# Two-layer gated cross-attention and feed-forward on one core: the negated mean moves to VectorE, the first feed-forward looks three tiles ahead instead of four, six chunks of the last weights are signed during the convolution, and loads change their places

## The chip, the cores and the metric

The kernel runs on one core of a Trainium2 chip. The core has TensorE (PE, matmuls), VectorE (DVE), ScalarE (ACT), GpSimd (POOL) and SyncE (SP, which here only issues DMA transfers); each runs its own instruction stream, and they meet by semaphores. The metric is the device time of one execution in microseconds (us).

## The reference, cut to what matters

`x` is 8x256x512, `ctx` has the same shape. Four residual steps follow each other:

```python
x = x + tanh(g_xattn[0]) * ssm_conv(ctx, ctx, layernorm(x), taps, D)      # causal conv of the pair products k_i*v_j, times q, summed over i
x = x + tanh(g_ffn[0])   * bitnet_ffn(layernorm(x), w1, w2, w3)           # hidden 1408, rows quantised to 8 bits, weights to {-1,0,1}/scale
x = x + tanh(g_xattn[1]) * masked_softmax_attention(layernorm(x), ctx)    # one head, 256 keys a batch
x = x + tanh(g_ffn[1])   * one_bit_ffn(layernorm(x), w1, w2, w3)          # hidden 2048, groups of 64 quantised, weights sign(w)*mean|w|
```

`layernorm(x) = (x - mean) / sqrt(var + 1e-5)` over the last axis. The mean of the absolute weights is over a whole matrix.

## The kernel before, in words

`x` lives on chip as 16 tiles of 128x512 (`x_sb[:, n, :]`). The four residual steps are four stages, each a loop over 16 tiles: the **convolution** (`n` = 0..15), the **first feed-forward** (`t` = 0..15), the **attention** (`i` = 0..15) and the **last feed-forward** (`n` = 0..15). Every engine has one stream, written out by hand in the order in which it runs; nothing reorders it, so a wait holds back everything behind it on its engine. Stages overlap only where the streams say so: the first tiles of a stage are prepared in the last steps of the stage before.

**Layer norm.** `ln_sums` (VectorE, L276 statistics and L278 aggregate, written as mean and variance), `ln_root` (GpSimd, L282 and L285) and, outside the convolution, `ln_norm` (GpSimd, L290, one 128x512 tensor_scalar that subtracts the mean and multiplies by the root). The convolution's own norm is on ScalarE (L867).

**Convolution.** For tile n, SyncE loads the filter matrices (`load_toeplitz`, L324, from `kpad`), x (L316) and the context heads (`load_context`, L313). GpSimd forms the pair products (`pairs`, L485 of 128x1536 and L488 of 128x256). TensorE runs two times 20 matmuls (L627) for a tile, transposes q (L615) and the result (L622). ScalarE's `copy_q` (L850, L852) takes the transposed q out of PSUM; in `conv(n)` TensorE turns q for n+1, and some 14 matmuls later it needs its copy. VectorE folds (L1069 to L1084). Beside it ScalarE takes the first feed-forward's weights in chunks: the absolute sums (`sum_weight`, L878, at the steps of `ABS_STEP`) and the ternary values (`ternary`, L885 and L888, at `TERN_STEP`).

**First feed-forward.** For tile t: three chunks of up-matmuls (L690, 24 instructions), their SiLU on ScalarE, `a_product` on VectorE (L1119), then quantising (`a_scale_h`, L1125), rounding, a DMA transpose, and 11 down-matmuls (L702). Its input is prepared ahead: `a_stats` (L276), `a_norm` (L290), `a_scale_x` (L1099 to L1106), `a_round_x`, `a_integers_x` (L521), `turn_x` (a DMA transpose). The order of these in the loop is t+4 for `a_stats` and `a_norm` and t+3 for `a_scale_x`.

**Last weights.** 24 chunks of 128x1024 are loaded by SyncE (`load_b`, L362) into two buffers, and ScalarE's `sign_b` writes the signs (L915) and the sum of the absolutes (L917). It begins in the fifth step of the first feed-forward and goes on through the attention, one a step, to the first steps of the last feed-forward.

**Attention.** For tile i: transposes (L713), scores (L724, from `load_rows` and `ctxT`), softmax with ScalarE's L926 and L933, readout (L746). Layer norm and input of the last feed-forward's first three tiles are also prepared here.

**Last feed-forward.** For tile n: 64 up-matmuls (L763), 32 down-matmuls (L780). The input of tile n+1 is prepared within step n: `fb_scale_x`, `fb_round_x`, `fb_deq_x`, `fb_high_x`, `fb_low_x`, and SyncE's `fb_turn_x` (L444, DMA transpose).

## Time and profile before

| what | value |
|---|---|
| median of 3 runs | 732.27 us (729.6 to 733.1) |
| the profiled execution | 732.03 us |
| its span in the trace | 730.2 us |
| busy: TensorE, VectorE, ScalarE, GpSimd | 693.4, 607.0, 372.4, 326.7 us |
| granted TensorE clock, mean | 0.993 |

A timeline row gives the start in us from the span's beginning, the length of the group in us, the engine, the line of the program, output and input, the count, and in brackets the idle time ahead of it with what ended it. "Busy" of one engine says how much it had to do, and not how much of that the others waited for.

### The profile page before, as it was taken

To read this page: it belongs to the slowest core of one execution; us is meant where nothing else is said; L and a number is where in the kernel's file an instruction comes from. 1 tells how busy PE (TensorE), PEld (TensorE's weight loads), DVE (VectorE), ACT (ScalarE), POOL (GpSimd) and SP (SyncE) were. 2 spreads that over 40 slices of the span, in tenths; PEclk is the share of its full clock that TensorE was granted. 3 is DMA by queue.
4 is the path that set the end of the run, shared out by engine and by line. 5 is a ranking of instruction groups with operands and counts; after the bars stand their busy time and mean duration, and the time that the engine had idled before them with its cause. 6 is when DMAs were issued, how large, how long until landed. Compare 5 with 4: busy or idle time off the path is not lost.

```text
span 730.2 us, 9410 instructions
## 1 busy us (share of the span) xinstructions
PE 693.4 (95%) x3162; PEld 388.4 (53%) x3162; DVE 607.0 (83%) x1094; ACT 372.4 (51%) x541; POOL 326.7 (45%) x362
## 2 busy tenths in 40 slices
PE   5999999988889999899989999999999999999897
PEld 3777777766534444466664444444444444444343
DVE  3998888898899998756985899988888888898871
ACT  3255976281366668546887644443444334433430
POOL 5679788878787665467870002211011111110000
PEclk9999999999999999999999999999999999999999
DMA  8563363320046878979554433334223343332133
GB/s 281 195 242 127 107 247 129 116 78 10 7 113 163 161 166 171 206 252 389 169 145 116 101 73 88 84 76 83 56 63 75 86 88 88 72 87 65 37 73 101
DMA packets 140288, 90.97 MB, mean 125 GB/s; under 512 B 118992, under 2 KB 118992, under 8 KB 140240
## 3 DMA queue, kind: packets, MB, share of 16 engines
q1 hardware_dynamic: 138512, 86.35, 44.1%
q0 software_dynamic: 1200, 3.93, 1.6%
q8 instruction: 25, 0.41, 0.2%
q14 instruction: 23, 0.19, 0.1%
q10 hardware_dynamic: 528, 0.09, 0.1%
HBM read 53.04 MB, written 8.47 MB: 84 GB/s over the span
## 4 chain that ended last, share of the span: by engine, by line
PE 65%; DVE 18%; POOL 6%; DMA 4%; ACT 4%; issue 3%; SPq 0%; POOLq 0%; ACTq 0%; DVEq 0%
PE psum L763 26%; PE psum L627 18%; PE psum L780 14%; DVE phase_space L1119 3%; DVE a_scalars L1125 3%; POOL phase_space L290 3%; PE psum L724 2%; PE psum L746 2%; DVE ln_bn L276 2%; DVE a_scalars L1106 1%; DMA phase_space<-in_L_weights 1%; DVE a_scalars L1099 1%; DVE x_sb L1137 1%; DMA x_sb<-x_between 1%; PE psum L615 1%
## 5 line engine op out<-in xcount | busy, mean ns | idle before, releaser
L763 PE MATMUL psum<-phase_space 128*128 128x512 f16 x1024 | 225.3, 381 | 3.9 <-DMA phase_space<-phase_space 3.2
L627 PE MATMUL psum<-phase_space 128*128 128x288 f32 x640 | 165.3, 414 | 14.3 <-DVE phase_space L1258 8.8
L763 PEld LDWEIGHTS psum<-phase_space 128*128 128x128 f16 x1024 | 100.2, 98 | 127.4 <-issue 4.7
L627 PEld LDWEIGHTS psum<-phase_space 128*128 128x128 f32 x640 | 121.3, 194 | 47.2 <-issue 8.8
L602 POOL DMA_DIRECT2D out<-x_sb x15 | 9.5, 630 | 293.9 <-DVE x_sb L1251 293.9
L780 PE MATMUL psum<-phase_space 128*128 128x512 f16 x512 | 112.6, 379 | 0.0
L290 POOL TENSOR_SCALAR phase_space<-x_sb,ln_ag,ln_rs 128x512 f32<-128x512 f32 x48 | 101.2, 2108 | 9.1 <-POOL ln_rs L285 7.4
L690 PE MATMUL psum<-phase_space 128*128 128x512 bf16 (+1 forms) x384 | 79.2, 361 | 4.7 <-DVE phase_space L1119 4.3
L780 PEld LDWEIGHTS psum<-phase_space 128*128 128x128 f16 x512 | 50.1, 98 | 60.4
L1024 ACT ACTIVATE phase_space<-psum,b_scalars 128x512 f32<-128x512 f32 x64 | 43.2, 681 | 74.6 <-PE psum L763 74.2
L1030 ACT ACTIVATE phase_space<-phase_space,magic 128x1024 f32<-128x1024 f32 x32 | 36.5, 1148 | 84.8 <-DVE phase_space L1230 84.8
L1218 DVE SCALAR_TENSOR_TENSOR phase_space<-psum,b_scalars,phase_space 128x512 f32<-128x512 f32 x64 | 47.6, 747 | 27.1 <-ACT phase_space L1024 26.4
L690 PEld LDWEIGHTS psum<-phase_space 128*128 128x128 bf16 x384 | 37.1, 98 | 45.4 <-DVE phase_space L1119 4.4
L1069 DVE TENSOR_TENSOR phase_space<-psum,phase_space 128x1024 f32<-128x1024 f32 x32 | 39.1, 1222 | 16.8 <-PE psum L627 16.6
L485 POOL TENSOR_TENSOR phase_space<-phase_space 128x1536 f32<-128x1536 f32 x16 | 48.6, 3040 | 3.5 <-DMA phase_space<-in_context_heads 3.5
L1173 DVE TENSOR_REDUCE phase_space<-phase_space 128x8 f32<-128x512 f32 (+1 forms) x32 | 47.3, 1479 | 0.6
L276 DVE BATCH_NORM_STATS2 ln_bn<-x_sb 128x6 f32<-128x512 f32 x64 | 43.4, 679 | 3.0 <-DMA x_sb<-x_between 2.9
L702 PE MATMUL psum<-phase_space 128*128 128x512 bf16 x176 | 41.2, 383 | 1.8 <-DMA phase_space<-phase_space 1.8
L1243 DVE TENSOR_TENSOR phase_space<-phase_space 128x512 f16<-128x512 f32 x64 | 39.8, 684 | 0.0
L1237 DVE SCALAR_TENSOR_TENSOR phase_space<-phase_space 128x1024 f32<-128x1024 f32 x32 | 37.8, 1223 | 1.3
L285 POOL TENSOR_TENSOR ln_rs<-ln_ve,neg_half 128x1 f32<-128x1 f32 x64 | 36.2, 566 | 5.3
L282 POOL TENSOR_SCALAR ln_ve<-ln_ag 128x1 f32<-128x1 f32 x64 | 13.2, 206 | 56.3 <-DVE ln_ag L278 54.0
(110 smaller groups left out, 1013.3 us busy)
## 6 DMA issues: line engine op xcount, KB each, us to landing
phase_space<-in_L_weights SPq DMA_DIRECT2D x24, 512.0 KB, 4.6
phase_space<-in_L_weights SPq DMA_DIRECT2D x12, 704.0 KB, 7.0
phase_space<-kpad SPq DMA_DIRECT2D x14, 512.0 KB, 4.1
phase_space<-in_context_heads SPq DMA_DIRECT2D x16, 384.0 KB, 4.8
x_sb<-in_x_tiles SPq DMA_DIRECT2D x16, 256.0 KB, 4.6
phase_space<-in_context_turned SPq DMA_DIRECT2D x8, 512.0 KB, 6.2
x_between<-x_sb SPq DMA_DIRECT2D x16, 256.0 KB
x_sb<-x_between SPq DMA_DIRECT2D x16, 256.0 KB, 6.1
```

The lines of the kernel that those rows point to most:

```text
L276: nc.vector.bn_stats(ln_bn[:, stage, n % 2, :], x_sb[:, n, :]).then_inc(s_ln[stage], 1)
L290: nc.gpsimd.tensor_scalar(dst, x_sb[:, n, :], ln_ag[:, stage, n, 0:1], ln_rs[:, stage, n:n + 1], ALU.subtract, ALU.mult).then_inc(s_done, 1)
L485: nc.gpsimd.tensor_tensor(at(kv_k, E, [[NP, rows], [E, 3], [1, E]]), at(cx_sb[k], 0, [[EX, rows], [0, 3], [1, E]]), at(cx_sb[k], 1, [[EX, ...
L627: last = nc.tensor.matmul(at(bank(4 * hh + lo), 0, [[64, B], [1, NP]]), toep[n % 2][:, hh, (lo - li) * P:(lo - li + 1) * P], kv[n % 2][:, ...
L690: last = nc.tensor.matmul(bank(UPA[c][part])[:, 0:w], fa_qT[t % 4][:, kk, :], a_wT[part][:, kk, c0:c0 + w], start=(kk == 0), stop=(kk == L ...
L702: last = nc.tensor.matmul(bank(6 + t % 2), fa_hT[t % 2][:, c, :], a_wT[2][:, c, :], start=(c == 0), stop=(c == JA - 1))
L763: last = nc.tensor.matmul(bank(2 * (m % 3) + w), fb_qT[n % 2][:, kk % 2, kk // 2, :], b_wT[w][:, kk // 2, c * 512:(c + 1) * 512], start=(k ...
L780: last = nc.tensor.matmul(bank(6 + k), fb_hT[k][:, part, c, :], b_wT[2][:, c, :], start=(c == 0 and part == 0), stop=(c == JB - 1 and part ...
L1024: nc.scalar.activation(fb_s[m % 2], bank(2 * (m % 3)), ACT.Silu, scale=fb_sm[:, n % 4, 2:3]).then_inc(g_si, 1)
L1173: nc.vector.tensor_reduce(gx[:, 0, :], grouped(src), AX.X, ALU.max, apply_absolute_value=True).then_inc(s_steps, 1)
L1218: nc.vector.scalar_tensor_tensor(fb_h[n % 2][:, c * 512:(c + 1) * 512], bank(2 * (m % 3) + 1), fb_sm[:, n % 4, 3:4], fb_s[m % 2], ALU.mult ...
L1243: nc.vector.tensor_tensor(fb_tp[n % 2][:, 1, g * 512:(g + 1) * 512], fb_t[n % 2][:, g * 512:(g + 1) * 512], fb_tp[n % 2][:, 0, g * 512:(g ...
```

## The change

1. `ln_nm`, the negated mean, is a third instruction of `ln_sums` on VectorE (128x1), for all stages but the convolution's; `ln_norm` then adds it and multiplies by the root, instead of subtracting the mean and multiplying.
2. The second pair product of tile 0 goes from GpSimd to VectorE. The filter pad's store moves behind the first loads. One sum of absolute weights goes from step 5 to step 4.
3. The first feed-forward prepares `a_stats` and `a_norm` three tiles ahead (before: four) and `a_scale_x` two (before: three); the last half fold of the convolution stands behind the first two products.
4. Six of the 24 chunks of the last weights are loaded at n = 9 to 15 of the convolution and signed in its steps 10, 11, 14 and 15. The other 18 keep two buffers and move earlier; none is left for the last feed-forward.
5. SyncE: `turn_hidden` ahead of `turn_x`, `load_rows(4)` and `load_rows(5)` earlier, the last chunks among `fb_turn_x`.
6. In the last feed-forward, the input of tile 15 is scaled at the end of step 13 and finished in the first half of step 14.

```diff
         def ln_sums(dve, stage, n):
+            done = LN_STEPS[stage] * n
...
+            if stage > 0:
+                dve.wait_ge(s_ln[stage], done + 2)
+                nc.vector.tensor_scalar(ln_nm[:, stage, n:n + 1], ln_ag[:, stage, n, 0:1], -1.0, None, ALU.mult
+                                        ).then_inc(s_ln[stage], 1)
...
-            nc.gpsimd.tensor_scalar(dst, x_sb[:, n, :], ln_ag[:, stage, n, 0:1], ln_rs[:, stage, n:n + 1],
-                                    ALU.subtract, ALU.mult).then_inc(s_done, 1)
+            nc.gpsimd.tensor_scalar(dst, x_sb[:, n, :], ln_nm[:, stage, n:n + 1], ln_rs[:, stage, n:n + 1],
+                                    ALU.add, ALU.mult).then_inc(s_done, 1)
...
+        ABS_STEP[1, 2] = 4
...
+        NBF = 6
+        B_STEP = {10: (0,), 11: (1, 2), 14: (3, 4), 15: (5,)}
...
                     if n + 2 < NT:
                         load_toeplitz(n + 2)
+                    for q in {9: (0, 1), 11: (2,), 12: (3, 4), 15: (5,)}.get(n, ()):
+                        load_b(q)
...
                 for t in range(NT + 1):
+                    if t >= 1:
+                        turn_hidden(t - 1)
                     if t < NT - 2:
                         turn_x(t + 2)
-                    if t >= 1:
-                        turn_hidden(t - 1)
...
-                load_b(6)
-                load_b(7)
+                load_rows(4)
+                load_b(13)
+                load_rows(5)
...
+                load_b(21)
                 fb_turn_x(0)
-                load_b(2 * PERW + 1)
+                load_b(22)
                 fb_turn_x(1)
-                for j in range(2 * PERW + 2, NBC):
-                    load_b(j)
+                load_b(23)
                 fb_turn_x(2)
...
                     if n >= NT - 3:
                         a_round_x(n + 3 - NT)
+                    for q in B_STEP.get(n, ()):
+                        sign_b(q)
...
                 for t in range(NT):
                     a_silu(t, 0)
                     if t >= 1:
                         a_round_h(t - 1)
                     a_silu(t, 1)
-                    if t < NT - 3:
-                        a_round_x(t + 3)
+                    if 1 <= t < NT - 2:
+                        a_round_x(t + 2)
...
-                    if i >= 3:
-                        sign_b(i + 3)
+                    if 4 <= i < 15:
+                        sign_b(i + 9)
...
-                        if NT + 3 + NCB * n + c < NBC:
-                            sign_b(NT + 3 + NCB * n + c)
...
                 for t in range(NT):
                     a_product(t, 0)
+                    if 1 <= t < NT - 2:
+                        a_scale_x(t + 2)
+                    a_product(t, 1)
+                    if t < NT - 3:
+                        a_stats(t + 3)
                     if t == 0:
-                        a_product(0, 1)
                         fold_heads(NT - 1, 1)
-                    if t < NT - 3:
-                        a_scale_x(t + 3)
-                    if t >= 1:
-                        a_product(t, 1)
-                    if t < NT - 4:
-                        a_stats(t + 4)
                     a_product(t, 2)
...
+                    if n == NT - 3:
+                        fb_scale_x(NT - 1)
+                        fb_up_scales(NT - 1)
```

What this makes of ScalarE's stream around the convolution's tiles 11 and 12. Before, behind the copy of q for tile 12 (its last two rows are ahead of the first shown) follow the norm, the copy of the result, and directly the copy of q for tile 13:

```order
L860 ACTIVATE phase_space<-phase_space 128x64x8 [waits conv_summed,context_loaded0]
L867 ACTIVATE phase_space<-x_sb,ln_off,ln_rs 128x512 [waits conv_x_transposed,conv_offset_done]
L874 ACTIVATE phase_space<-psum,gates 128x512 [waits residual0_done,result_transposed]
L850 ACTIVATE phase_space<-psum 128x64x8 [waits products_folded,conv_x_transposed]
L852 ACTIVATE phase_space<-psum 128x64x4
L860 ACTIVATE phase_space<-phase_space 128x64x8 [waits conv_summed,context_loaded1]
L867 ACTIVATE phase_space<-x_sb,ln_off,ln_rs 128x512 [waits conv_x_transposed,conv_offset_done]
L874 ACTIVATE phase_space<-psum,gates 128x512 [waits residual0_done,result_transposed]
L885 ACTIVATE phase_space<-phase_space,magic,a_inv 128x1408 [waits a_means]
```

After the change, from the same place (L885, L892, L899, L875, L877 are the former L860, L867, L874, L850, L852; L941 and L943 are the sign and the absolute sum):

```order
L885 ACTIVATE phase_space<-phase_space 128x64x8 [waits conv_summed,context_loaded0]
L892 ACTIVATE phase_space<-x_sb,ln_off,ln_rs 128x512 [waits conv_x_transposed,conv_offset_done]
L899 ACTIVATE phase_space<-psum,gates 128x512 [waits residual0_done,result_transposed]
L941 ACTIVATE phase_space<-phase_space 128x1024 [waits b_weight_loaded1]
L943 ACTIVATE phase_space,b_abs<-phase_space 128x1024 [waits b_weight_signed]
L941 ACTIVATE phase_space<-phase_space 128x1024 [waits b_weight_loaded0]
L943 ACTIVATE phase_space,b_abs<-phase_space 128x1024 [waits b_weight_signed]
L875 ACTIVATE phase_space<-psum 128x64x8 [waits products_folded,conv_x_transposed]
L877 ACTIVATE phase_space<-psum 128x64x4
L885 ACTIVATE phase_space<-phase_space 128x64x8 [waits conv_summed,context_loaded1]
```

Two chunks of the last weights, four instructions, stand between the copy of the result and the copy of q for tile 13; the second pair waits for the load of the chunk q = 2.

SyncE's stream at the same place. Before, the filter load for tile 13 (first row) and what follows to tile 15's:

```order
L324 DMA phase_space<-kpad 128x2x512 [waits conv_summed]
L313 DMA phase_space<-in_context_heads 128x768 [waits squares_ready,pairs_ready]
L324 DMA phase_space<-kpad 128x2x512 [waits conv_summed]
L313 DMA phase_space<-in_context_heads 128x768 [waits squares_ready,pairs_ready]
L324 DMA phase_space<-kpad 128x2x512 [waits conv_summed]
```

After (L338 is the former L324, L327 the former L313, L380 the load of a chunk):

```order
L338 DMA phase_space<-kpad 128x2x512 [waits conv_summed]
L380 DMA phase_space<-in_L_weights 128x1024 [waits b_weight_summed]
L327 DMA phase_space<-in_context_heads 128x768 [waits squares_ready,pairs_ready]
L338 DMA phase_space<-kpad 128x2x512 [waits conv_summed]
L380 DMA phase_space<-in_L_weights 128x1024 [waits b_weight_summed] x2
L327 DMA phase_space<-in_context_heads 128x768 [waits squares_ready,pairs_ready]
L338 DMA phase_space<-kpad 128x2x512 [waits conv_summed]
```

The chunk q = 2 is issued behind the filter load for tile 13, and the chunks 3 and 4 behind that for tile 14.

VectorE's stream at the start of the first feed-forward. Before, from the statistics of tile 3's input on:

```order
L276 BN_STATS ln_bn<-x_sb 128x6
L278 BN_AGGR ln_ag<-ln_bn 128x2
L1299 TENSOR_TENSOR a_down<-a_mean,gates 128x1
L1119 SCALAR_TENSOR_TENSOR phase_space<-psum,a_scalars,phase_space 128x512 x2
L1084 TENSOR_TENSOR phase_space<-phase_space 128x32x16
L1099 TENSOR_REDUCE a_scalars<-phase_space 128x1
L1102 TENSOR_SCALAR a_scalars<-a_scalars 128x1
L1105 RECIPROCAL a_scalars<-a_scalars 128x1
L1106 TENSOR_SCALAR a_scalars<-a_mean,a_scalars 128x2
L276 BN_STATS ln_bn<-x_sb 128x6
```

After (L1149 is the former L1119, L1114 the former L1084, L281 and L283 the statistics, L286 the negated mean, L1155 the maximum of the hidden row):

```order
L1334 TENSOR_TENSOR a_down<-a_mean,gates 128x1
L1149 SCALAR_TENSOR_TENSOR phase_space<-psum,a_scalars,phase_space 128x512 x2
L281 BN_STATS ln_bn<-x_sb 128x6
L283 BN_AGGR ln_ag<-ln_bn 128x2
L286 TENSOR_SCALAR ln_nm<-ln_ag 128x1
L1114 TENSOR_TENSOR phase_space<-phase_space 128x32x16
L1149 SCALAR_TENSOR_TENSOR phase_space<-psum,a_scalars,phase_space 128x384
L1155 TENSOR_REDUCE a_scalars<-phase_space 128x1
L1158 TENSOR_SCALAR a_scalars<-a_scalars 128x1
L1161 RECIPROCAL a_scalars<-a_scalars 128x1
L1162 TENSOR_TENSOR a_scalars<-a_scalars,a_down 128x1
```

The statistics of tile 3 stand behind the first two products instead of ahead of them, the last half fold (L1084, L1114) behind these, and the scaling of tile 3's input (L1099 to L1106) is no longer between the fold and the third product.

## Rows read from the trace of the kernel before

**Rows 1.** The page: the chain that ended last, and the last feed-forward's up-matmuls.

```profile
PE 65%; DVE 18%; POOL 6%; DMA 4%; ACT 4%; issue 3%; SPq 0%; POOLq 0%; ACTq 0%; DVEq 0%
...
L763 PE MATMUL psum<-phase_space 128*128 128x512 f16 x1024 | 225.3, 381 | 3.9 <-DMA phase_space<-phase_space 3.2
```

**Rows 2.** TensorE's waits by line and releaser: us in total, times, longest.

```profile
PE psum L690 <- DVE phase_space L1119: 4.3, 3, 1.7
...
PE psum L713 <- POOL phase_space L290: 4.2, 3, 2.1
...
PE psum L627 <- POOL phase_space L488: 4.0, 2, 2.1
...
PE psum L627 <- ACT phase_space L852: 1.5, 1, 1.5
...
PE psum L763 <- DVE phase_space L1218: 0.7, 1, 0.7
```

**Rows 3.** ScalarE's timeline, end of step 5: start, length, instruction.

```profile
77.61 1.36 ACT L878 ACTIVATE phase_space<-phase_space 128x1408 bf16<-128x1408 f32 x1
...
78.97 0.57 ACT L850 ACTIVATE phase_space<-psum 128x512 f32<-128x512 f32 x1
...
79.44 0.37 ACT L852 ACTIVATE phase_space<-psum 128x256 f32<-128x256 f32 x1
```

**Rows 4.** TensorE's timeline in the convolution: start, length of the group.

```profile
140.49 5.02 PE L627 MATMUL psum<-phase_space 128*128 128x288 f32 x20
...
176.21 4.14 PE L627 MATMUL psum<-phase_space 128*128 128x288 f32 x9 [1.88 <-POOL phase_space L488]
```

**Rows 5.** SyncE's timeline, the filter load for n=13.

```profile
140.25 0.38 SPq L324 DMA_DIRECT2D phase_space<-kpad  x1
```

**Rows 6.** The line that loads the last weights, from issue to landing.

```profile
DMA to landing us min/median/max: 3.4/4.6/9.0
```

**Rows 7.** ScalarE's timeline in the attention, rows around signs of weights.

```profile
339.68 1.06 ACT L915 ACTIVATE phase_space<-phase_space 128x1024 f16<-128x1024 f32 x1 [2.64 <-DMA phase_space<-in_L_weights]
...
375.65 1.05 ACT L915 ACTIVATE phase_space<-phase_space 128x1024 f16<-128x1024 f32 x1
...
377.69 0.19 ACT L917 ACTIVATION_READ_ACCUMULATOR phase_space<-phase_space 128x1 f32 x1
```

**Rows 8.** Busy time by stretch: PE, PEld, DVE, ACT, POOL, granted clock.

```profile
160.00:180.00 20.00, 16.00 (x63) 11.94 (x62) 18.52 (x25) 6.59 (x9) 18.25 (x17) 0.92 0.12 34
214.00:290.00 76.00, 76.00 (x376) 36.45 (x375) 73.03 (x148) 52.34 (x67) 51.12 (x51) 1.00 0.76 159
```

**Rows 9.** GpSimd's timeline, end of the convolution.

```profile
168.73 2.08 POOL L290 TENSOR_SCALAR phase_space<-x_sb,ln_ag,ln_rs 128x512 f32<-128x512 f32 x1
...
176.24 0.62 POOL L521 TENSOR_SCALAR phase_space<-phase_space 128x512 bf16<-128x512 f32 x1
```

**Rows 10.** VectorE's timeline, start of the first feed-forward.

```profile
187.92 0.15 DVE L1102 TENSOR_SCALAR a_scalars<-a_scalars 128x1 f32<-128x1 f32 x1
...
196.07 0.69 DVE L1099 TENSOR_REDUCE a_scalars<-phase_space 128x1 f32<-128x512 f32 x1 [0.81 <-POOL phase_space L290]
...
210.54 0.94 DVE L1106 TENSOR_SCALAR a_scalars<-a_mean,a_scalars 128x2 f32<-128x2 f32 x1
```

**Rows 11.** TensorE's timeline, start of the first feed-forward.

```profile
188.15 3.62 PE L690 MATMUL psum<-phase_space 128*128 128x512 bf16 x16
...
199.16 1.47 PE L690 MATMUL psum<-phase_space 128*128 128x384 bf16 x8 [1.72 <-DVE phase_space L1119]
...
209.37 2.55 PE L702 MATMUL psum<-phase_space 128*128 128x512 bf16 x11 [0.59 <-DMA phase_space<-phase_space]
```

**Rows 12.** TensorE's timeline, attention's start and last feed-forward's end.

```profile
308.76 0.66 PE L713 MATMUL psum<-ident,phase_space 128*128 128x128 f32 x4 [2.15 <-POOL phase_space L290]
...
309.25 3.03 PE L724 MATMUL psum<-phase_space 128*128 128x256 f32 x8
...
329.20 1.96 PE L724 MATMUL psum<-phase_space 128*128 128x256 f32 x8 [1.03 <-issue]
...
682.59 7.76 PE L763 MATMUL psum<-phase_space 128*128 128x512 f16 x29 [2.87 <-DMA phase_space<-phase_space]
```

**Rows 13.** SyncE's timeline, transposes ahead of the last feed-forward.

```profile
373.23 1.26 SPq L444 DMA_TRANSPOSE phase_space<-phase_space  x1
...
679.83 1.23 SPq L444 DMA_TRANSPOSE phase_space<-phase_space  x1
```

116 lines of the change are left out of this document (71 added, 45 removed).

## Prediction

> **What bounds the kernel now.** I read four views. First the chain that ended last [rows 1]: TensorE holds 65% of it and VectorE 18%, GpSimd, DMA and ScalarE 4 to 6% each. So TensorE is what the kernel runs at, and the rest is stalls that others give it. Second, TensorE's waits [rows 2], which name the stalls: the first feed-forward's up-matmuls wait 4.3 us for products, the attention's transposes 4.2 us for GpSimd's norm, the convolution 4.0 us for GpSimd's pairs and 1.5 us for ScalarE's copy of q. Third, the timelines around each of them, since every part of this change acts on the work ahead of one such place, and not on the steady tiles. Fourth, the granted clock [rows 8]: it is 0.92 in the stretch from 160 to 180 us, which holds the stalls at the convolution's end, and 9 matmuls there take 4.14 us, where 20 take 5.02 us at tile 12 [rows 4]. Nine should take 2.26 us, so the low level of the clock (1.2 instead of 2.4 GHz for a while) adds 1.9 us to a stall. Of the two stalls at the convolution's end only the second shows this, so a stall of about 2 us brings it at some times and not at others.
>
> **The base.** The sum is made against the profiled execution, 732.03 us (a span of 730.2 and 1.8 around it), which is 0.24 us below the median of the runs.
>
> **Start of the program: 0.** VectorE takes a 128x256 product that GpSimd did in under 1 us; both are on the way to the first fold and the matmuls. The pad's store is behind loads, but the filter for tile 2 is wanted long after. I take nothing; the ends are 0.1 us less and 0.4 us more.
>
> **One sum of weights less in step 5: -1.35.** ScalarE ends its last sum of 1.36 us, and copies q in 0.84 us [rows 3], for which TensorE waits 1.5 us [rows 2]. With one sum gone the copy is 1.36 us earlier, and the wait is nearly gone. In step 4 ScalarE has room.
>
> **The chunks in the convolution: +6.6, and this is the largest term.** The order shows that the sign of chunk q = 2 stands ahead of the copy of q for tile 13, and that SyncE issues the load of this chunk only behind the filter load for tile 13. That filter load waits until tile 11's matmuls have left their buffer, and is issued at 140.25 us [rows 5]. So the chunk's load is issued at 140.25 + 0.42 = 140.7. It lands after 3.4 to 9.0 us, 4.6 in the median [rows 6]; beside the filter's own 512 KB I take 4.8: 145.5. Sign, absolute sum and the read of the accumulator take 377.69 + 0.19 - 375.65 = 2.2 us [rows 7], to 147.7, and the copy 0.84, to 148.6. TensorE starts tile 12 at 140.49 and wants the copy after 14 of the first 20 matmuls, 140.49 + 0.7 x 5.02 = 144.0 [rows 4]. It stalls 4.6 us (3.2 with the quickest landing, 8.8 with the slowest), and the clock adds up to 1.9 us; with a landing near the median I put the two at 6.6 (rounded up by 0.1 for the context load between). The other chunks (0 and 1 loaded a step earlier, 3 and 4 two steps ahead of step 14) are in time and their 2.2 us fit into ScalarE's idle time; chunk 5 in step 15 delays the first SiLU, which is counted below.
>
> **The norm on GpSimd.** The 128x512 subtract and multiply takes 2.08 us. Another tensor_scalar of that engine on as many elements, add and multiply, takes 0.62 us [rows 9]. It differs in three things: add for subtract, immediates for the two 128x1 scalars, and bf16 output. I cannot tell them apart in this trace. The bounds are 0.62 and 2.08 us, and I take 0.7: of the three, the subtraction is the one that the change takes away and that concerns every element. The 48 negated means cost VectorE an instruction of the kind of L1102, 0.15 us [rows 10], with the semaphore some 0.2 us. L1102 (one column in and out) takes 0.15 us in all its 16 places, while L1106 of two columns takes 0.94 us when GpSimd is at work, so it waits. I count the negated mean, one column, with the former; had it to wait like the latter, that is rival six. The Trainium skill, SBUF — State Buffer, section "Who interferes with whom", speaks against this part of the change: tensor_scalar is among the operations that can take the ports shared with GpSimd, and whoever comes second is blocked for the whole instruction. By that rule alone the sum would be that of rival six; that it needs more than one column is what the rows of L1102 say, and not that section.
>
> - End of the convolution: of the two stalls for the pairs, 4.0 us together [rows 2], the first is behind a norm on GpSimd's queue and shrinks by 1.4; the second follows a pair product that waits for VectorE, and stays: **-1.4**.
> - Start of the attention: TensorE waits 2.15 us for the norm of tile 1 [rows 12], and 1.4 of it goes. The scores after it take 3.03 us, where 8 such take 1.96 later [rows 12], so a clock fall of 1.1 to 1.3 goes with it: **-2.7**.
>
> **Start of the first feed-forward: -4.6.** From the first up-matmul at 188.15 to the first down-matmul at 209.37 there are 21.2 us [rows 11], of which the waits for products are 4.3 [rows 2], those for the transpose 0.6 and a small one 0.3: 5.2, so TensorE has 16.0 us of work. On VectorE's path to the third product of tile 0 lies the scaling of tile 3's input with a wait of 0.81 us for the norm, from 196.07 to some 197.5, and a like block for tile 4 a little later [rows 10]. The first of these leaves the stretch (2.2 us with its wait), the statistics too go behind the first products, and the waits of the second vanish with a quicker norm. Against it stand the SiLU that is 2.2 us late for chunk 5, and the last half fold that now waits for two products. Walking the order with these durations, the third product is done at about 195.5 and the down-matmuls start 16.6 us behind the first up-matmul: 0.6 of the 5.2 us is left. Bounds: 0 and 5.2.
>
> **The steady tiles: 0** for the first feed-forward, where TensorE is busy for 76.00 of 76 us and VectorE for 73.03 [rows 8]. These are some 10.7 tiles, 76 us by the 24 up- and 11 down-matmuls of each, so VectorE has 0.28 us to spare in a tile; the negated mean takes 0.2 of it, and the waits for GpSimd's slower norms, which count as busy, come back. If these don't fall, it becomes the bound (rival two).
>
> **End of the first feed-forward: +1.4.** Its last input is scaled a tile later, and SyncE issues the reloads of x for the attention behind one more transpose, 1.2 to 1.3 us each [rows 13]; the statistics of the attention's first tile are later by that much. I take 1.4, from 0 to 2.5.
>
> **The rest of the attention: +1.5.** The stall of 1.03 us ahead of tile 4's scores, which wait for their rows, goes since that load is moved up: **-1.1** [rows 12]. The negated means make the two steps in which VectorE is full longer: **+0.5**. Chunk 22 is issued behind the transpose for tile 0 of the last feed-forward, at 373.23 + 1.26 and the issue time [rows 13], lands near 379, and ScalarE wants it in step 13, before at 375.65 [rows 7]. That is a wait like that of 2.64 us at 339.68; the copy for the next scores stands behind it: **+2.1** (0 to 3.5).
>
> **The last feed-forward: -0.7 and -2.6.** No signs are left in its first tiles: VectorE's product, late by 0.7 us for ScalarE [rows 2], is on time. At its end the input of tile 15 is scaled at the end of step 13 and not within step 14, so its transpose, issued at 679.83 [rows 13], goes out about 1.4 us earlier and shortens the wait of 2.87 us [rows 12]. The 29 matmuls behind it take 7.76 us, while 1024 take 225.3, 6.4 for 29 [rows 1]; a stall of half the length should spare most of this 1.4: 1.4 + 1.2.
>
> **Sum.** 0 - 1.35 + 6.6 - 1.4 - 2.7 - 4.6 + 1.4 + 1.5 - 0.7 - 2.6 = -3.85: **728.2 us**, which is 0.55% under the median. A measurement of this kernel can tell about 0.5% (3.7 us) from no change, so this lies on the edge of it.
>
> **The rivals.**
> 1. *Forecast*, 728.2, on its own 724.5 to 732: the stall at tile 12 eats what the starts of two stages win. Chance 0.50.
> 2. *The norm stays at 2.08 us* and the cost is in the scalars from memory. Then the 1.4 and 2.7 are not won, 2.4 of the 4.6 are lost again, and the 0.2 us a tile on VectorE, which has 0.28 to spare on average, but not evenly, add some 0.14 x 13 = 1.8: 728.2 + 8.3 = 736.5, slower. For it: every one of the 48 norms has two pointers, every fast one none. Against it: one value a partition is a small thing to fetch for 512 elements. It decides from about 1.9 us a norm up. Chance 0.20.
> 3. *Chunk 2 lands as late as the slowest* (9.0 us), since the filter for 13, the chunk, the context and the weights share the queue: +4.2, 732.4. Against it: the slowest landings stand in the attention, with more loads in flight. Chance 0.10.
> 4. *No stall at tile 12*, since the copy of q has more slack than I read or the chunk is there: 728.2 - 6.6 = 721.6. Against it: the orders of two engines, which leave no other reading. Chance 0.08.
> 5. *The first feed-forward's start wins nothing*: chunk 5 holds the first SiLU, and the fold the third product: 732.8. Chance 0.07.
> 6. *The negated mean waits for GpSimd*, as L1106 does: of its 0.94 us some 0.75 are wait, and half of that, 0.4, in each of the 13 steady tiles of the first feed-forward, where VectorE has no room: +5.2, 733.4. Chance 0.05.
>
> **How the numbers follow.** The time is that of the forecast. The range reaches to rival 4 below and rival 2 above, 721.5 to 737, which leaves out the outer halves of both and what none foresees. Faster by over 0.5% (below 728.6): 0.32 of the first, all of the fourth, 0.02 of the fifth, 0.42. Within: 0.15 of the first, 0.04 of the second, 0.07 of the third, 0.05 each of the last two, 0.36. Slower (above 735.9): 0.03, 0.16 and 0.03 of the first three, 0.22.
>
> **What would show it.** In the trace of the changed kernel: a wait of 3 to 9 us of TensorE within tile 12 that ends with the copy of q, with ScalarE's sign waiting for a DMA ahead of it; the norm at 0.6 to 0.8 us; the negated mean at 0.15; no wait at 79 us; the first down-matmul 16 to 17.5 us after the first up-matmul; a wait in the attention's step 14 or 15 that ends with ScalarE; the last transposed tile's wait at 1.3 to 1.8 us. The prediction is wrong if the norm is not faster, or if TensorE passes tile 12 without a stall.

## The result and the profile after

The changed kernel takes 738.0 us (median of 5 runs, 737.5 to 740.1), the kernel before 732.0: a ratio of 1.0101 over all runs, interval 1.0076 to 1.0126 (the two medians alone give 1.0082). It is about 1% slower; forecast were 728.2. The page of the changed kernel, with busy time, the chain by engine (from 18% to 24% for VectorE, from 6% to 1% for GpSimd, against [rows 1]) and the line of the norm:

```profile
PE 695.2 (94%) x3150; PEld 387.8 (53%) x3162; DVE 613.5 (83%) x1143; ACT 372.3 (51%) x541; POOL 263.3 (36%) x361
...
PE 62%; DVE 24%; DMA 4%; ACT 4%; issue 3%; SPq 1%; POOL 1%; ACTq 0%; DVEq 0%; POOLq 0%
...
L299 POOL TENSOR_SCALAR phase_space<-x_sb,ln_nm,ln_rs 128x512 f32<-128x512 f32 x48 | 39.3, 820 | 12.3 <-POOL ln_rs L294 7.6
```

The norm is now 0.77 us in the median (0.82 the mean), with two 128x1 pointers and f32 output as before: GpSimd is 63 us less busy than before. What TensorE waits for (us in total, times, longest), against [rows 2]:

```profile
PE psum L652 <- ACT phase_space L877: 4.8, 1, 4.8
...
PE psum L749 <- ACT phase_space L952: 4.0, 3, 2.6
...
PE psum L715 <- DVE phase_space L1149: 3.9, 5, 1.9
```

The copy of q has gone from 1.5 to 4.8 us, the attention's scores behind ScalarE (L749, before L724) from 1.9 to 4.0, and the products (L1149) are nearly as before.

To see where the time went, the same instructions are compared in both traces. TensorE's timeline before (start, length, count; L615 the transpose of q, L702 down-matmuls of tiles 7 and 13, L724 the scores of tile 1, L763 the first of the last feed-forward):

```profile
161.21 0.60 PE L615 MATMUL psum<-ident,phase_space 128*128 128x128 f32 x4
...
259.27 2.54 PE L702 MATMUL psum<-phase_space 128*128 128x512 bf16 x11
...
303.63 2.55 PE L702 MATMUL psum<-phase_space 128*128 128x512 bf16 x11 [0.24 <-DMA phase_space<-phase_space]
...
315.04 1.89 PE L724 MATMUL psum<-phase_space 128*128 128x256 f32 x8
...
384.17 3.62 PE L763 MATMUL psum<-phase_space 128*128 128x512 f16 x16
```

and after (L640, L715, L727, L749 and L788 are the former L615, L690, L702, L724 and L763):

```profile
147.11 3.25 PE L652 MATMUL psum<-phase_space 128*128 128x288 f32 x6 [4.78 <-ACT phase_space L877]
...
167.08 0.60 PE L640 MATMUL psum<-ident,phase_space 128*128 128x128 f32 x4
...
191.69 3.40 PE L715 MATMUL psum<-phase_space 128*128 128x512 bf16 x15
...
209.83 2.54 PE L727 MATMUL psum<-phase_space 128*128 128x512 bf16 x11
...
234.88 4.91 PE L715 MATMUL psum<-phase_space 128*128 128x512 bf16 x23 [0.68 <-DVE phase_space L1149]
...
261.42 2.54 PE L727 MATMUL psum<-phase_space 128*128 128x512 bf16 x11
...
265.87 4.91 PE L715 MATMUL psum<-phase_space 128*128 128x512 bf16 x24 [1.92 <-DVE phase_space L1149]
...
309.09 2.55 PE L727 MATMUL psum<-phase_space 128*128 128x512 bf16 x11 [0.90 <-DMA phase_space<-phase_space]
...
317.65 1.89 PE L749 MATMUL psum<-phase_space 128*128 128x256 f32 x8
...
386.68 2.70 PE L749 MATMUL psum<-phase_space 128*128 128x256 f32 x8 [2.62 <-ACT phase_space L952]
...
392.13 3.62 PE L788 MATMUL psum<-phase_space 128*128 128x512 f16 x16
```

| stretch (its end, before and after) | forecast | measured |
|---|---|---|
| start, to the transpose of q at the head of tile 12 (140.05, 138.33) | -1.35 | -1.7 |
| tiles 12 and 13 with the stall (161.21, 167.08) | +6.6 | +7.6 |
| to the first up-matmul (188.15, 191.69) | -1.4 | -2.3 |
| to the first down-matmul (209.37, 209.83) | -4.6 | -3.1 |
| tiles 0 to 13 (303.63, 309.09) | +1.4 | +5.0 |
| to the scores of tile 1 (315.04, 317.65) | -2.7 | -2.9 |
| to the last feed-forward's first matmul (384.17, 392.13) | +1.5 | +5.4 |
| last feed-forward (end, 730.2, 736.2) | -3.3 | -2.0 |
| sum | -3.85 | +6.0 |

All eight rows have the sign of the forecast, and six are within about 1.5 us of it. Two hold 7.5 of the 9.85 us between forecast and result: the tiles of the first feed-forward, and the attention. Within them, 4.4 of the 5.0 us are lost by tile 11, where I had put 0, and the 5.4 us lie behind the scores of tile 14 (378.61 against 376.19, still 0.2 us less than at tile 1), so at the attention's end.

### The profile page after: what moved, and what is told of

Read it like the earlier page. It is cut to its first block, busy times and chain, and to the rows that moved or that the text cites. A ratio compares the mean times of both kernels' runs of the same rounds, so it can differ in the third digit from the quotient of the medians.

```text
span 736.2 us, 9448 instructions
## 1 busy us (share of the span) xinstructions
PE 695.2 (94%) x3150; PEld 387.8 (53%) x3162; DVE 613.5 (83%) x1143; ACT 372.3 (51%) x541; POOL 263.3 (36%) x361
## 4 chain that ended last, share of the span: by engine, by line
PE 62%; DVE 24%; DMA 4%; ACT 4%; issue 3%; SPq 1%; POOL 1%; ACTq 0%; DVEq 0%; POOLq 0%
PE psum L788 24%; PE psum L652 17%; PE psum L805 14%; DVE phase_space L1149 3%; DVE a_scalars L1155 3%; PE psum L771 3%; DVE ln_bn L281 2%; PE psum L749 2%; DMA phase_space<-in_L_weights 1%; DVE phase_space L1203 1%; DVE phase_space L1114 1%; DVE a_scalars L1129 1%; DVE a_scalars L1136 1%; DVE phase_space L1248 1%; DVE x_sb L1167 1%
## 5 line engine op out<-in xcount | busy, mean ns | idle before, releaser
L788 PE MATMUL psum<-phase_space 128*128 128x512 f16 x1024 | 224.3, 379 | 2.9 <-DMA phase_space<-phase_space 2.0
L652 PE MATMUL psum<-phase_space 128*128 128x288 f32 x640 | 165.8, 415 | 16.6 <-DVE phase_space L1288 8.6
L788 PEld LDWEIGHTS psum<-phase_space 128*128 128x128 f16 x1024 | 99.7, 98 | 125.8 <-DVE phase_space L1248 2.8
L715 PE MATMUL psum<-phase_space 128*128 128x512 bf16 (+1 forms) x377 | 79.7, 361 | 5.1 <-DVE phase_space L1149 3.9
L715 PEld LDWEIGHTS psum<-phase_space 128*128 128x128 bf16 x384 | 36.2, 98 | 48.0 <-DVE phase_space L1149 6.1
L1099 DVE TENSOR_TENSOR phase_space<-psum,phase_space 128x1024 f32<-128x1024 f32 x32 | 39.1, 1222 | 22.6 <-PE psum L652 22.5
L281 DVE BATCH_NORM_STATS2 ln_bn<-x_sb 128x6 f32<-128x512 f32 x64 | 43.7, 683 | 1.5 <-DMA x_sb<-x_between 1.5
L299 POOL TENSOR_SCALAR phase_space<-x_sb,ln_nm,ln_rs 128x512 f32<-128x512 f32 x48 | 39.3, 820 | 12.3 <-POOL ln_rs L294 7.6
L727 PE MATMUL psum<-phase_space 128*128 128x512 bf16 x171 | 40.0, 379 | 2.7 <-DMA phase_space<-phase_space 2.5
L935 ACT ACTIVATE phase_space<-phase_space,magic,a_scalars 128x1408 f32<-128x1408 f32 x16 | 25.0, 1561 | 30.0 <-DVE a_scalars L1161 30.0
```

The costliest lines, as they stand in the source:

```text
L281: nc.vector.bn_stats(ln_bn[:, stage, n % 2, :], x_sb[:, n, :]).then_inc(s_ln[stage], 1)
L299: nc.gpsimd.tensor_scalar(dst, x_sb[:, n, :], ln_nm[:, stage, n:n + 1], ln_rs[:, stage, n:n + 1], ALU.add, ALU.mult).then_inc(s_done, 1)
L652: last = nc.tensor.matmul(at(bank(4 * hh + lo), 0, [[64, B], [1, NP]]), toep[n % 2][:, hh, (lo - li) * P:(lo - li + 1) * P], kv[n % 2][:, ...
L715: last = nc.tensor.matmul(bank(UPA[c][part])[:, 0:w], fa_qT[t % 4][:, kk, :], a_wT[part][:, kk, c0:c0 + w], start=(kk == 0), stop=(kk == L ...
L727: last = nc.tensor.matmul(bank(6 + t % 2), fa_hT[t % 2][:, c, :], a_wT[2][:, c, :], start=(c == 0), stop=(c == JA - 1))
L788: last = nc.tensor.matmul(bank(2 * (m % 3) + w), fb_qT[n % 2][:, kk % 2, kk // 2, :], b_wT[w][:, kk // 2, c * 512:(c + 1) * 512], start=(k ...
```

## The experiments

All ratios are to the kernel before, run beside each; it took 731.6 to 732.5 us there. The changed kernel's 738.0 us were measured beside 732.0. So a difference of two medians that were not measured side by side is good to about 1 us. Lengths of stretches are read from one profiled execution of each kernel, and are differences of starts in TensorE's timeline.

**The negated mean alone.** The kernel before, with `ln_nm` on VectorE and the norm as add, multiply, and nothing else of the change.

```diff
+            if stage > 0:
+                dve.wait_ge(s_ln[stage], done + 2)
+                nc.vector.tensor_scalar(ln_nm[:, stage, n:n + 1], ln_ag[:, stage, n, 0:1], -1.0, None, ALU.mult)
...
-            ... ln_ag[:, stage, n, 0:1], ln_rs[:, stage, n:n + 1], ALU.subtract, ALU.mult)
+            ... ln_nm[:, stage, n:n + 1], ln_rs[:, stage, n:n + 1], ALU.add, ALU.mult)
```

> The kernel before with one part of the change alone: the negated mean on VectorE and add, multiply on GpSimd. Theory A (VectorE is the bound of the steady feed-forward tiles, and the negated mean costs what it takes there): tiles at about 7.26 to 7.28 us instead of 7.13, a stall of TensorE near the mask's maximum in tile 8, together +3 to +4.4; the quicker norm gives back 2.8 at the attention's start, 1 to 2 at the convolution's end and about 1 at the feed-forward's start. Sum about 731, 729 to 733. Theory B (the shorter look-ahead costs the steady tiles, not the negated mean): steady tiles at 7.13 and a time of about 727.

Measured: 730.2 us, ratio 0.9988 (0.9972 to 1.0005). Tiles 0 to 6 stay at 7.13 us, and from tile 7 on the loss comes, with a stall of 1.59 us at tile 8. So the negated mean does cost the feed-forward (tiles 0 to 13 take 95.6 us, 94.3 before) and the attention more (71.5 us from the scores of tile 1 to the last feed-forward, 69.1 before), and the two nearly eat what the quick norm wins elsewhere. The time is theory A's, but the pitch of 7.28 was not there from tile 1 on, as A had said: before, VectorE runs so far ahead that some tiles can be longer for it.

**No negated mean in the first feed-forward.**

```diff
-        LN_STEPS = (2, 3, 3, 3)
+        LN_STEPS = (2, 2, 3, 3)
...
+            if stage == 1:      # the norm as before
+                nc.gpsimd.tensor_scalar(dst, ..., ln_ag[...], ln_rs[...], ALU.subtract, ALU.mult)
```

> The changed kernel, with the first feed-forward's norm back to subtract, multiply without a negated mean (the other stages keep it). Theory A: steady tiles at 7.13, no stall at tile 8, -4.4; at the convolution's end and the feed-forward's start the slower norm costs 1 to 2: about 735.5. Theory B: the steady loss stays, and the time is 738 to 740.

Measured: 738.9 us, ratio 1.0098 (1.0067 to 1.0129). The number is theory B's, but its trace is A's. TensorE's first up-matmul, first down-matmul and the down-matmul of tile 13 in this kernel:

```profile
195.48 3.40 PE L719 MATMUL psum<-phase_space 128*128 128x512 bf16 x15
...
214.17 2.54 PE L731 MATMUL psum<-phase_space 128*128 128x512 bf16 x11
...
309.92 2.55 PE L731 MATMUL psum<-phase_space 128*128 128x512 bf16 x11 [0.76 <-DMA phase_space<-phase_space]
```

From the first down-matmul to tile 13's are 95.8 us; 99.3 in the changed kernel and 94.3 before. So 3.5 of the 5.0 us came back, at 7.13 us a tile and without a stall at tile 8. They were lost ahead of it: the first up-matmul is 3.8 us later than in the changed kernel, behind longer waits for pairs (GpSimd's queue with the slow norm), a low clock, and a landing of chunk 2 that was 1 us longer. A time alone would have misled here. The 3.5 us are not the price of the negated mean alone: with the slow norm the first down-matmul comes 18.7 us after the first up-matmul, and VectorE forms the maximum of tile 7 some 10.4 us ahead of that tile's down-matmuls, against 8.8 in the changed kernel; what that lead does is told in the next section.

**Chunk 2 loaded a tile earlier.**

```diff
-                    for q in {9: (0, 1), 11: (2,), 12: (3, 4), 15: (5,)}.get(n, ()):
+                    for q in {9: (0, 1), 10: (2,), 12: (3, 4), 15: (5,)}.get(n, ()):
```

> The changed kernel with the load of chunk q = 2 issued one tile earlier, behind the filter load for tile 12. Theory A (the sign that waits for its load holds the copy of q): no stall of TensorE in tile 12, -7.6, less a clock fall that may come back at the convolution's end (1.9): 730.5 to 732.5. Rival: the stall is made by ScalarE's amount of work or by a load that lands late wherever it is issued: 735 or more.

Measured: 731.4 us, ratio 0.9999 (0.9981 to 1.0018): 6.6 less. TensorE does not wait in tile 12, and tiles 12 and 13 take 21.16 us as before. Without this one load behind the wrong wait, the changed kernel takes as long as the kernel before.

**Chunks 22 and 23 ahead of the transposes.**

```diff
                 load_b(21)
+                load_b(22)
                 fb_turn_x(0)
-                load_b(22)
+                load_b(23)
                 fb_turn_x(1)
-                load_b(23)
```

> The changed kernel with the loads of chunks 22 and 23 issued ahead of the transposes of tiles 0 and 1 of the last feed-forward. Theory A (the chunk is late only because SyncE is held by the transpose): ScalarE's wait of 4.15 us in the attention's step 13 goes, TensorE's stall of 2.6 us and the low clock behind it too: -3.8 to -5.5, 732.5 to 734. Rival (the tail of the attention is bound by VectorE or the loads' own time): within 1 us of 738.

Measured: 734.4 us, ratio 1.0036 (1.0015 to 1.0057): 3.6 less, near the lower end of A. The stall of 2.62 us ahead of the last scores is gone, and from the scores of tile 1 to the last feed-forward there are 70.4 us (74.5 in the changed kernel, 69.1 before).

**Both.**

The two edits above together, without another.

> The changed kernel with both late loads mended: chunk 2 a tile earlier, and chunks 22 and 23 ahead of the transposes. The two stalls lie in stages that do not touch, so theory A adds them: 738.0 - 6.6 - 3.6 = 727.8 (726.5 to 729). Rival (what one mend wins is partly the same time as the other's, or another wait takes its place): 730 to 731.

Measured: 726.1 us, ratio 0.9918 (0.9897 to 0.994): 11.9 less than the changed kernel, and somewhat more than the sum, 10.2. They add; the last us and a half fits the clock (mean 0.999 against 0.993). In the traces each single mend has a place at the low clock that the changed kernel has not, or less of: the 20 matmuls behind the last stall of the convolution take 6.81 us with chunks 22 and 23 earlier (5.12 in the changed kernel), and the last eight scores 3.78 us with chunk 2 earlier (2.70). With both, neither is there. TensorE's down-matmuls of tiles 0 and 13 in it:

```profile
201.98 2.54 PE L727 MATMUL psum<-phase_space 128*128 128x512 bf16 x11
...
301.08 2.55 PE L727 MATMUL psum<-phase_space 128*128 128x512 bf16 x11 [0.77 <-DMA phase_space<-phase_space]
```

**The negated mean on GpSimd**, between variance and root, with both loads mended.

```diff
         def ln_root(pool, stage, n):
+            if stage > 0:
+                nc.gpsimd.tensor_scalar(ln_nm[:, stage, n:n + 1], ln_ag[:, stage, n, 0:1], -1.0, None, ALU.mult
+                                        ).then_inc(s_rs[stage], 1)
```

> Both loads mended, and the negated mean formed on GpSimd between the variance and the root, no longer on VectorE. Theory A (VectorE is the bound of the steady feed-forward tiles in the changed kernel, whose start gives it no head start): the steady tiles go back to 7.13, the stall at tile 8 goes or shrinks; 3 to 4.4 less than with both loads mended, 723.5 to 725. Rival (GpSimd's longer chain makes its norms late): within 1 us of it.

Measured: 720.8 us, ratio 0.9848 (0.9825 to 0.9871), the fastest kernel of this study; 5.3 less than with it on VectorE, more than A had said. Only 1.0 of it lies in tiles 0 to 13 of the first feed-forward (99.1 us with it on VectorE, 98.1 on GpSimd). Span against span it is 4.7 less (723.8, 719.1): 2.0 by the last down-matmul of the first feed-forward (312.88, 310.90), and 2.7 behind that, in the attention, where two statistics stand in a step. VectorE's step there is 3.9 to 4.0 us before, 4.35 in the changed kernel and 3.9 here, when TensorE's is 4.1.

**The mask's maximum from tile 8 to tile 14.**

```diff
-                    if t == 8:
+                    if t == NT - 2:
                         dve.wait_ge(c_mk, 16)
```

> Both loads mended, and VectorE's maximum over the mask (2.5 us) moved from tile 8 to tile 14 of the first feed-forward. Theory A: what VectorE does in a steady tile reaches TensorE one to one, so the stall of 1.9 us at tile 8 goes; at tile 14 it stands beside waits for DMA: 1 to 1.9 less. Rival: within 0.5 us.

Measured: 726.3 us, ratio 0.9927 (0.9905 to 0.995): nothing won against 726.1. The stall at tile 8 is gone and tile 13's down-matmul comes 1.3 us earlier, but the work is wanted at the attention's start too, where it makes a stall and brings the clock down. Its first scores:

```profile
306.05 3.60 PE L749 MATMUL psum<-phase_space 128*128 128x256 f32 x8 [1.47 <-ACT phase_space L952]
```

Eight matmuls take 3.60 us, where they take 1.89 in the rows above. Theory A was right for the place and wrong that tile 14 is free.

**The negated mean twice**, a copy and then the negation, in the first feed-forward only.

```diff
+            if stage == 1:
+                nc.vector.tensor_scalar(ln_cp[:, n:n + 1], ln_ag[:, stage, n, 0:1], 1.0, None, ALU.mult)
+                ... wait ...
+                nc.vector.tensor_scalar(ln_nm[:, stage, n:n + 1], ln_cp[:, n:n + 1], -1.0, None, ALU.mult)
```

> Both loads mended, and in the first feed-forward the mean is copied and then negated, two dependent 128x1 instructions for one. Theory A: some 0.2 us more a tile in tiles 0 to 12, pitch 7.28 to about 7.49, +2.5. Theory B (the negated mean is hidden and the shorter look-ahead costs): within 0.5 us.

Measured: 731.1 us, ratio 0.9986 (0.9971 to 1.0001), +5.0. The tiles take 7.47 us, and tiles 0 to 13 are 2.8 us longer (101.9 against 99.1), as A has it. Another 1.7 us are lost ahead of them (the first down-matmul at 203.68 against 201.98). Of these 1.0 lies at the very start of the program, where the first 14 matmuls take 6.16 us against 5.28 and no negated mean is formed, so it is no price of this edit; 0.7 lies behind it, where the last convolution tiles form statistics of this stage too. Theory B, in which it costs nothing, is out.

**Look-ahead of before, on the fastest kernel**: statistics and norm four tiles ahead, scaling three, and the order of the transposes as before.

```diff
-                    if 1 <= t < NT - 2:
-                        a_scale_x(t + 2)
-                    a_product(t, 1)
-                    if t < NT - 3:
-                        a_stats(t + 3)
+                    if t == 0:
+                        a_product(0, 1)
+                        fold_heads(NT - 1, 1)
+                    if t < NT - 3:
+                        a_scale_x(t + 3)
+                    if t >= 1:
+                        a_product(t, 1)
+                    if t < NT - 4:
+                        a_stats(t + 4)
```

> The best kernel so far (both loads mended, negated mean on GpSimd: 720.8) with the orders of the first feed-forward as before the change: statistics and norm four tiles ahead, scaling three, transposes of x ahead of those of h. Theory C (an earlier start only takes VectorE's head start away, since VectorE works without a break from then on): the first down-matmul comes 1.5 to 2.5 us later behind the first up-matmul, but the steady tiles lose 3 us less, above all at tile 8, so the time is within 1.5 us of 720.8. Rival (what the start wins stays): 722.5 to 724.

Measured: 721.8 us, ratio 0.9863 (0.9838 to 0.9888), 0.9 us from the fastest. The time is theory C's. Of its reasons, the later down-matmul (2.2 us) and the shorter tiles (3.3 us) are there, but tile 8 gives only a quarter of a us of it; and 2.1 us are lost again in the attention, among it a wait of 1.63 us for ScalarE ahead of a readout, where the fastest kernel's longest of that kind is 0.39; theory C did not name this. In the next section its trace is read.

**The negated mean on GpSimd, on the kernel before.**

```diff
-            nc.vector.tensor_scalar(ln_nm[:, stage, n:n + 1], ..., -1.0, None, ALU.mult)    # in ln_sums
+            nc.gpsimd.tensor_scalar(ln_nm[:, stage, n:n + 1], ..., -1.0, None, ALU.mult)    # in ln_root
```

> The kernel before with the norm as add, multiply and the negated mean formed on GpSimd instead of VectorE. With the negated mean on VectorE it took 730.2. Theory A (the negated means cost VectorE time that reaches TensorE in the feed-forward and the attention): 3 to 5 less, 725.5 to 727. Rival (they cost it only where the start is early): 729.5 to 730.5.

Measured: 727.2 us, ratio 0.9933 (0.9915 to 0.9951): 3.0 less than with it on VectorE by the medians, 4 by the two ratios, as theory A has it; the rival is out.

**Tile 15 prepared within step 14 again, on the fastest kernel.**

```diff
-                    if n == NT - 3:
-                        fb_scale_x(NT - 1)
-                        fb_up_scales(NT - 1)
...
-                    if 2 <= n < NT - 2:
+                    if 2 <= n < NT - 1:
                         fb_scale_x(n + 1)
                         fb_up_scales(n + 1)
```

> The best kernel so far (720.8) with the input of the last feed-forward's tile 15 prepared within step 14 again. If the earlier scaling is what shortened the wait for its transpose from 2.87 to 1.74 us and spared the clock fall behind it: +1.1 to +2.5, 722 to 723.3. Rival (the quicker norm or the absence of signs did that): within 0.5 us.

Measured: 722.6 us, ratio 0.9871 (0.9849 to 0.9893), +1.8. The wait for the transpose is 2.89 us as before ([rows 12]) against 1.74 in the changed kernel, and the 64 matmuls behind it, 15.31 us before, are slow again:

```profile
674.18 15.67 PE L788 MATMUL psum<-phase_space 128*128 128x512 f16 x64 [2.89 <-DMA phase_space<-phase_space]
```

So this part of the change is worth some 1.8 us in this kernel, 1.1 of them the wait.

**Three stretches side by side** (us, from the traces): from the first up-matmul to the first down-matmul, tiles 0 to 13, and the scores of tile 1 to the last feed-forward.

| kernel | start | tiles 0 to 13 | attention |
|---|---|---|---|
| before | 21.2 | 94.3 | 69.1 |
| before, negated mean on VectorE | 19.8 | 95.6 | 71.5 |
| before, negated mean on GpSimd | 19.6 | 94.9 | 68.1 |
| changed | 18.1 | 99.3 | 74.5 |
| both loads mended | 18.1 | 99.1 | 70.1 |
| and negated mean on GpSimd (fastest) | 17.5 | 98.1 | 67.2 |
| and look-ahead of before | 19.7 | 94.8 | 69.4 |

From VectorE to GpSimd, in both pairs, the tiles gain 0.7 to 1.0 us and the attention 2.8 to 3.4: the larger part of what the negated mean costs is paid in the attention. What makes the tiles long in the kernels with the new order is above all that order with its early start: restoring the old one gives back 3.3 us of them, at 2.2 us more in the start.

## Why the prediction was wrong

Two steps failed: the steady tiles of the first feed-forward, put at 0, where 4.4 us were lost by tile 11; and the attention behind its first tiles, put at +1.5 with +2.1 for chunk 22, where 5.4 were lost. A third, the start of the first feed-forward, won 3.1 us for 4.6.

**The stall at tile 12: right, and 1.0 us too small.** ScalarE's row after: it is done at 136.28, waits 7.79 us for chunk 2, and copies q behind it.

```profile
144.06 1.06 ACT L941 ACTIVATE phase_space<-phase_space 128x1024 f16<-128x1024 f32 x1 [7.79 <-DMA phase_space<-in_L_weights]
```

SyncE issues the chunk behind the filter load:

```profile
138.53 0.38 SPq L338 DMA_DIRECT2D phase_space<-kpad  x1
...
138.97 0.69 SPq L380 DMA_DIRECT2D phase_space<-in_L_weights  x1
```

From the issue to the sign are 5.1 us (I had put 4.8), and TensorE goes on at 147.11 after 4.78 us of wait (I had 4.6). The rest is the clock, as it was at 176 us before: behind the stall the matmuls and transposes of the tile take 2.8 us more than in rest, where I had counted 1.9 and rounded the sum up by 0.1. Chunk 2 a tile earlier took it away.

**The norm: right.** 0.77 us. Of the three differences that I could not tell apart, the bf16 output and the immediates are out, since the f32 output and the two pointers are as before; the subtraction is what is left, but for the column that the first pointer reads, which changed with it and was not tested by itself. The Trainium skill, GPSIMD Engine Reference, section 3.1, has 768 ns as the best case of a tight loop over 512 elements; the 0.77 us of this row agree with it, and the 2.08 us of the subtraction lie far above. Whether either instruction runs such a loop no run shows. The attention's start won 2.9 us, with the clock, where 2.7 were forecast.

**The steady tiles at 0: the first step that failed.** I had argued that VectorE had 0.28 us to spare in a tile, and that the waits for slow norms would come back. Neither holds; the tiles to 11 cost 4.4 us more. VectorE's rows after, from tile 2's maximum to tile 3's, and at tiles 7 and 8:

```profile
215.58 1.62 DVE L1155 TENSOR_REDUCE a_scalars<-phase_space 128x1 f32<-128x1408 f32 x1
...
221.93 0.18 DVE L283 BATCH_NORM_AGGREGATE ln_ag<-ln_bn 128x2 f32<-128x6 f32 x1
...
222.15 0.15 DVE L286 TENSOR_SCALAR ln_nm<-ln_ag 128x1 f32<-128x1 f32 x1
...
222.22 0.61 DVE L1149 SCALAR_TENSOR_TENSOR phase_space<-psum,a_scalars,phase_space 128x384 f32<-128x384 f32 x1
...
222.86 1.62 DVE L1155 TENSOR_REDUCE a_scalars<-phase_space 128x1 f32<-128x1408 f32 x1
...
252.61 1.62 DVE L1155 TENSOR_REDUCE a_scalars<-phase_space 128x1 f32<-128x1408 f32 x1
...
262.53 2.28 DVE L1354 TENSOR_REDUCE valid<-phase_space 128x8 f32<-128x2048 uint8 x1
```

Aggregate to product is 0.29 us, where it was 0.10 (L278 to L1119), and the maxima of two tiles (L1155) are 7.28 us apart without a pause. Before they were 7.07 apart without a pause too: the 3 us that [rows 8] seem to leave free were the gap between 7.07 and TensorE's 7.13, and the hundredths between rows. And the waits that were to come back were not for the norm. Before, in tile 4:

```profile
224.83 0.79 DVE L1106 TENSOR_SCALAR a_scalars<-a_mean,a_scalars 128x2 f32<-128x2 f32 x1
```

```profile
224.23 1.36 POOL L527 TENSOR_SCALAR phase_space<-phase_space 128x1408 bf16<-128x1408 f32 x1 [0.34 <-ACT phase_space L910]
```

VectorE's 128x2 instruction ends at 225.62, when GpSimd's rounding of the hidden row ends (225.59); its norm (L290) had ended 2.4 us earlier. After the change it is the same pair (L1136 and L551, both to 227.9), and the 128x2 instruction takes 0.79 us in the median as before. The mean itself never waits for GpSimd, in 48 of 48:

```profile
L286 DVE TENSOR_SCALAR ln_nm<-ln_ag x48: 153/153/155, 161.0 to 405.6; 128x1 f32<-128x1 f32 x48
```

This is what [rows 10] had said, and rival six, the one by the Trainium skill's rule on the shared ports (SBUF — State Buffer, "Who interferes with whom"), is out for one column of this kind of instruction; the section lets tensor_scalar take the shared ports only when its operands meet conditions, which I had passed over. The negated mean's cost was not a port, but the plain 0.19 us with its semaphore on an engine that was full: 0.7 to 1.0 us in tiles 0 to 13 and 2.8 to 3.4 in the attention, where I had put +0.5 for all steps. On GpSimd instead it gives back 5.3 us in all.

Another one-column instruction does wait, and with it comes the stall of 0.68 us at 234.88, which I had not foreseen:

```profile
232.06 1.36 DVE L1162 TENSOR_TENSOR a_scalars<-a_scalars,a_down 128x1 f32<-128x1 f32 x1
```

```profile
231.51 1.90 POOL L611 TENSOR_SCALAR phase_space<-phase_space 128x2048 f32<-128x2048 uint8 x1
```

The first takes 0.14 us in the median, and here ends with GpSimd's one instruction on the mask (233.42 and 233.41). Before, that instruction (L586) met a 128x2 one of VectorE that ended with it (0.37 us), and TensorE did not wait.

**A start that is won can be lost again.** The largest single piece of the loss in tiles 0 to 13 is the mask's maximum at tile 8, 2.3 us on VectorE. It was there before and cost TensorE nothing; I did not see that an early start takes away what hid it. What hides it is how long before the down-matmuls of a tile VectorE forms its maximum. For tile 7, before (VectorE's row; the down-matmuls start at 259.27 above):

```profile
248.56 1.62 DVE L1125 TENSOR_REDUCE a_scalars<-phase_space 128x1 f32<-128x1408 f32 x1
```

10.7 us ahead, and no stall at tile 8. After: 252.61 and 261.42, 8.8 us, and a stall of 1.92. The lead is 8.8 us in six of the first eight tiles there, where TensorE's tiles are as long as VectorE's (7.28): it has nothing left to give. In the fastest kernel, VectorE's row and then TensorE's first up-matmul, first down-matmul, tile 7's, the stall in tile 8, and the last down-matmul:

```profile
243.26 1.62 DVE L1155 TENSOR_REDUCE a_scalars<-phase_space 128x1 f32<-128x1408 f32 x1
```

```profile
184.15 4.92 PE L715 MATMUL psum<-phase_space 128*128 128x512 bf16 x23
...
201.61 2.54 PE L727 MATMUL psum<-phase_space 128*128 128x512 bf16 x11
...
252.29 2.54 PE L727 MATMUL psum<-phase_space 128*128 128x512 bf16 x11
...
256.31 4.92 PE L715 MATMUL psum<-phase_space 128*128 128x512 bf16 x24 [1.48 <-DVE phase_space L1149]
...
310.90 2.55 PE L727 MATMUL psum<-phase_space 128*128 128x512 bf16 x11 [0.26 <-DMA phase_space<-phase_space]
```

and in the same kernel with the look-ahead of before:

```profile
244.51 1.62 DVE L1154 TENSOR_REDUCE a_scalars<-phase_space 128x1 f32<-128x1408 f32 x1
```

```profile
183.96 3.40 PE L714 MATMUL psum<-phase_space 128*128 128x512 bf16 x15
...
203.61 2.55 PE L726 MATMUL psum<-phase_space 128*128 128x512 bf16 x11 [0.59 <-DMA phase_space<-phase_space]
...
253.97 2.55 PE L726 MATMUL psum<-phase_space 128*128 128x512 bf16 x11 [0.26 <-DMA phase_space<-phase_space]
...
257.73 4.91 PE L714 MATMUL psum<-phase_space 128*128 128x512 bf16 x24 [1.22 <-DVE phase_space L1148]
...
309.67 2.55 PE L726 MATMUL psum<-phase_space 128*128 128x512 bf16 x11 [0.23 <-DMA phase_space<-phase_space]
```

Their leads are 9.0 and 9.5 us and their stalls 1.48 and 1.22: lead and stall make 10.5 to 10.7 us in all four kernels. In the changed kernel the start won 3.1 us, a third less than the 4.6 that I had worked out: 18.1 us where I had put 16.6, since waits of 0.24 to 0.90 us for VectorE are left. In these two kernels it is 17.5 and 19.7 us. But at the last down-matmul the kernel with the late start is ahead, 309.67 against 310.90. Of the 3.2 us that it catches up, a quarter of a us lies at tile 8, and 2.3 are waits of the down-matmuls of tiles 11 to 13 for the transposed hidden rows (0.52, 1.15 and 0.94 us in the early one, 0.33 in the late one); then it falls behind again in the attention. Whether the look-ahead or the order of the transposes on SyncE makes these is open, since this kernel restored both.

**Chunk 22 at +2.1: the second step, mis-sized.** The wait was forecast in place and cause; what was missing is what follows it:

```profile
383.63 1.06 ACT L941 ACTIVATE phase_space<-phase_space 128x1024 f16<-128x1024 f32 x1 [4.15 <-DMA phase_space<-in_L_weights]
```

```profile
378.13 1.26 SPq L465 DMA_TRANSPOSE phase_space<-phase_space  x1
...
379.44 0.57 SPq L380 DMA_DIRECT2D phase_space<-in_L_weights  x1
```

The chunk is issued at 379.44 and signed at 383.63. ScalarE waits 4.15 us, where 3.5 was my upper end, and TensorE 2.62 us of it, 0.5 more than the 2.1 that I had put. The rest of what the stretch lost is what I had left out. Behind the stall the scores, the transpose and the readout run at the low clock, 1.7 us longer than before (2.70 us for eight scores against 1.89 in rest), which I had counted for the other stalls and not here. Ahead of it a small matmul waits 0.69 us for VectorE's total (L843 for L1385); that wait is in no kernel that forms the negated mean elsewhere, before included, so it belongs to the +0.5. Chunks 22 and 23 earlier gave 3.6 us back.

**The last feed-forward: -2.0 for -3.3.** The wait went from 2.87 to 1.74 us, 1.1 less, where 1.4 was forecast. Of the 1.3 us that the low clock had cost behind it, 0.56 are now a wait for VectorE at the last chunk of the same tile, which I had not counted. VectorE's late product in the first tiles (0.7 us) is on time, but the first three tiles are only 0.3 us shorter for it.

**The chances.** What came true is none of the rivals as written: slower by 1%, at 0.22. The high end of my range (737.0) was made from single rivals; two stretches that were each too small by over 3.5 us went past it. The signs that I had named held for the stall at tile 12, the norm, the negated mean, the wait at 79 us, the one at the attention's end and the last transposed tile; the one of the first down-matmul, 16 to 17.5 us after the first up-matmul, failed with 18.1.

## What to carry to other kernels

A spare tenth of a microsecond on an engine that shows no pause is not spare: compare its pitch with that of the bound engine, and put a new small instruction with its semaphore (0.19 us here) on the path. Before a load is put into a queue, look at what stands ahead of it there and when that is released: the loads behind the wrong entries cost 10 to 12 us in this kernel, and moving them gave it back. A stage that starts earlier can have less lead for its one-off work; read the lead (here the row maximum against the down-matmul) before and after.

## What the hardware showed that I had not expected

GpSimd's 128x512 tensor_scalar takes 2.08 us with a subtraction first and 0.77 with an addition; the column that the first scalar is read from is the only other difference. Stalls of 1.5 to 2.6 us at the attention's first or last scores were followed by TensorE's low clock in all five traces that had one (8 matmuls in 2.70 to 3.78 us, 1.89 in rest). One of 1.82 us in its tile 14 before (at 373.98) was not, and those of 1.9 to 2.4 us at the convolution's end were so in three traces (20 matmuls in 6.81 us against 5.12) and not in the others. A VectorE instruction of one column took 1.36 us instead of 0.14 while GpSimd worked on 128x2048, when the negated mean, one column too but with one input, took 0.15 in all 48 places.
